# Last sequence of a hybrid Mamba, FFN and minGRU layer: the squares of both feed-forward blocks are summed on TensorE instead of on GpSimd

## The reference

```
x = x + mamba(layernorm(x))          # 256 inner channels, 16 states, conv of 4 taps
x = x + ffn(layernorm(x))            # block "a" in the kernel
x = x + min_gru_block(layernorm(x))  # 512 wide
x = x + ffn(layernorm(x))            # block "d", the same weights as "a"

def ffn(x):                          # ternary weights, 128 -> 512 -> 128
    h = gelu(ternary_linear(x, w_up))
    return ternary_linear(h, w_down)

def ternary_linear(x, w):
    rms = sqrt(sum(x * x, axis=-1)) / sqrt(d)
    return (x / (rms + 1e-8)) @ w_q.T
```

## Time and profile before

| | |
|---|---|
| median of 3 runs | 870.47 us (866.34 to 874.72) |
| the profiled execution | 870.38 us |
| its span, first to last instruction | 868.6 us |
| PE busy | 706.7 us (81%) |
| DVE busy | 677.0 us (78%) |
| ACT busy | 641.6 us (74%) |
| POOL busy | 590.9 us (68%) |
| mean granted TensorE clock | 0.904 |
| POOL L593, all 8 units | x48, 61.1 us, 1273 ns each |

### The profile page before, as it was taken

One profiled execution on the slowest core, in us unless ns is written; L12 is line 12 of the kernel. 1 busy time (PEld: TensorE's weight loads), 2 busy tenths in 40 slices (PEclk: granted clock), 3 DMA queues, 4 the chain that ended last, 5 costly groups with the idle time before them and its releaser, 6 DMA issues. The chain is left out here.

```text
span 868.6 us, 12461 instructions
## 1 busy us (share of the span) xinstructions
PE 706.7 (81%) x4060; PEld 594.6 (68%) x4060; DVE 677.0 (78%) x1059; ACT 641.6 (74%) x966; POOL 590.9 (68%) x375
## 2 busy tenths in 40 slices
PE   6446664789878997999788987999789977996975
PEld 5234553668767885778676876788667866785764
DVE  4379988869987998879977998799888997753231
ACT  4775669697789968996879778987898479616313
POOL 3178967776778877787868697888777576615312
PEclk9685776889989998999889998999899979999996
DMA  2541221112111211121111211121112111000000
GB/s 47 146 143 45 74 74 49 51 48 63 37 41 44 89 39 47 39 67 56 37 51 47 75 37 50 38 74 37 49 38 73 50 36 38 13 1 2 13 1 12
DMA packets 35185, 42.79 MB, mean 49 GB/s; under 512 B 7457, under 2 KB 17074, under 8 KB 35122
## 3 DMA queue, kind: packets, MB, share of 16 engines
q1 hardware_dynamic: 35122, 42.00, 15.9%
HBM read 39.63 MB, written 2.36 MB: 48 GB/s over the span
## 5 line engine op out<-in xcount | busy, mean ns | idle before, releaser
L441 POOL TENSOR_TENSOR inflow<-dtu,b_all 128x1024 f32<-128x1024 f32 x127 | 307.4, 2424 | 85.9 <-DVE state L1006 53.4
L1006 DVE TENSOR_TENSOR_SCAN state<-dA,inflow 128x512 f32<-128x512 f32 x256 | 298.4, 1207 | 31.2 <-ACT dA L771 27.8
L771 ACT ACTIVATE dA<-dt,decay_c 128x512 f32<-128x512 f32 x256 | 169.8, 685 | 56.6 <-DVE state L1006 55.7
L1023 DVE TENSOR_TENSOR state<-state,c_ps 128x1024 f32<-128x1024 f32 x128 | 155.5, 1215 | 22.4 <-PE c_ps L1305 18.8
L1314 PE MATMUL y_ps<-ident,state 128*128 128x128 f32 x1024 | 151.2, 297 | 0.0
L1314 PEld LDWEIGHTS y_ps<-ident,state 128*128 128x128 f32 x1024 | 135.7, 156 | 11.9 <-issue 3.8
L1201 PE MATMUL work<-in_hi,wzh_hi 128*128 128x512 f32 x256 | 103.6, 405 | 5.6 <-issue 4.3
L1305 PE MATMUL c_ps<-xd,pick 128*128 128x512 f32 x128 | 65.0, 508 | 46.0 <-DVE state L1023 45.7
L1203 PE MATMUL work<-in_lo,wzh_hi 128*128 128x512 f32 x256 | 101.0, 394 | 0.0
L1202 PE MATMUL work<-in_hi,wzh_lo 128*128 128x512 f32 x256 | 101.0, 394 | 0.0
L593 POOL TENSOR_TENSOR wide<-wide 128x512 f32<-128x512 f32 x48 | 61.1, 1273 | 27.5 <-ACT wide L818 25.0
(11 more groups left out here) (166 smaller groups left out, 1491.6 us busy)
## 6 DMA issues: line engine op xcount, KB each, us to landing
b_all<-b_scratch SPq DMA_DIRECT2D x128, 256.0 KB, 3.1
x_tok<-in_x SPq DMA_DIRECT2D x8, 256.0 KB, 3.8
out_x<-x_tok SPq DMA_DIRECT2D x8, 256.0 KB, 3.7
wide<-in_Wz SPq DMA_DIRECT2D x1, 1024.0 KB, 6.4
wide<-in_Wh SPq DMA_DIRECT2D x1, 1024.0 KB, 8.7
skip_f<-in_W SPq DMA_DIRECT2D x2, 256.0 KB, 5.7
dtu<-in_W_in SPq DMA_DIRECT2D x1, 256.0 KB
b_scratch<-gated SPq DMA_DIRECT2D x8, 32.0 KB, 1.6
```

The lines of the kernel that those rows point to most:

```text
L441: eng.tensor_tensor(inflow[:, n % 2, :, tok(b)], dtu[:, :, tok(b)], b_all[:, n % RING, tok(b)].unsqueeze(1).broadcast_to([P, HALVES, TO[b] ...
L771: act.activation(dA[:, h, tok(b)], dt[:, b % 2, h, tok(b)], ACT.Exp, scale=decay_c[:, h, n:n + 1]).then_inc(s_dA[h], 1)
L1006: dve.tensor_tensor_scan(state[:, g % 3, h, tok(b)], dA[:, h, tok(b)], inflow[:, n % 2, h, tok(b)], first, ALU.mult, ALU.add).then_inc(s_s ...
L1023: dve.tensor_tensor(state[:, g % 3, :, tok(b)], state[:, g % 3, :, tok(b)], c_ps[:, tok(b)].unsqueeze(1).broadcast_to([P, HALVES, TO[b] - ...
```

## The change

For t = N - 1 = 7 alone, POOL's `ffn_sum` does nothing, in both blocks. PE's `ffn_sumsq` of that unit multiplies all four blocks of squares by the column of ones and accumulates in PSUM: 4 blocks times 4 token tiles are 16 products, which are 32 matmuls with 32 weight loads. It waits for each square in turn on `s_sq[c]` instead of once on `s_sqsum[c]`. For the other units the count of products stays 4; only their start flag is now set on the first alone.

```
             def ffn_sum(t, c, k):
+                if t == N - 1:
+                    return
                 pool.wait_ge(s_sq[c], FB * t + k + 1)
...
             def ffn_sumsq(t, c):
                 p = c + ".sumsq"
-                pe.wait_ge(s_sqsum[c], 3 * t + 3)
+                if t < N - 1:
+                    pe.wait_ge(s_sqsum[c], 3 * t + 3)
                 bank_free(t, p)
-                for j in tiles(t):
-                    last = pe.matmul(bank(p)[:, j:j + 1], square[:, 0, cols(j)], ones[:, 0:1], start=True, stop=True)
+                terms = FB if t == N - 1 else 1
+                for k in range(terms):
+                    if t == N - 1:
+                        pe.wait_ge(s_sq[c], FB * t + k + 1)
+                    for j in tiles(t):
+                        last = pe.matmul(bank(p)[:, j:j + 1], square[:, k, cols(j)], ones[:, 0:1],
+                                         start=(k == 0 and j == tiles(t)[0]), stop=(k == terms - 1),
+                                         skip_group_check=True)
                 last.then_inc(*made(p))
```

## The result

| | before | changed |
|---|---|---|
| median of 6 runs | 870.41 us (866.34 to 875.53) | 884.11 us (874.96 to 889.6) |
| ratio | | 1.0123, 95% interval 1.0065 to 1.0182 |
| the profiled execution | 870.38 us, span 868.6 | 889.6 us, span 887.2 |
| mean granted clock | 0.904 | 0.889 |

The kernel became slower by 13.7 us in the median and by 1.2% in the ratio (10.7 us), where +4.8 us had been forecast. The range ended at 880.0.

The account below looks back on a forecast made before the run. PE was taken as the engine on the path in both blocks of unit 7, POOL's sums as hidden. Block "a" 2.15 plus block "d" 2.68 gave 4.83 us on 870.38 us, so 875.2 us, range 870.4 to 880.0.

Parts of the forecast that it names:

- What bounds the place: Unit 7, both blocks: PE's queue holds the products with ones; POOL's sums are ready 1.15 and 0.32 us earlier.
- The price of the pairs and the waits: Unit 7's sums on PE: 24 added pairs cost 2.68 us a block; the waits cost 0, at most 0.1 us.
- the bound of 0.211: Added pairs at the half clock: 0.211 us each, 5.1 us for 24, from part 0 of the down projection.
- Block "a" on the path, 2.15 us: Unit 7, block "a": 0.53 us of the added 2.68 is absorbed before DVE's read, 2.15 us go through.
- Both partners of the stretch behind it: Behind block "a": POOL's root and unit 6's sums and products all shift by 2.15 us; no slack takes it back.
- Block "d", 2.68 us: Unit 7, block "d": part 1 of the down projection and DVE's last operation start 2.68 us later; up to 5.1 plus.
- Rival B: The clock stays low through the end: +7.0 us in block "d", +9.2 with block "a", 879.6 us; chance 0.09.
- The forecast's own sign of being wrong: At the program's end: among the listed signs, a granted clock of 0.50 beyond 866 us would show the forecast wrong.
- Rival A: POOL's sums were the bound in unit 7: -1.42 us in block "a", +0.45 in "d", 869.4 us; chance 0.06.
- Rival C: Unit 7's added products are nearly free, weight loads hidden: 870.4 us; chance 0.05.

Follow-up runs that it names:

- e5: The changed kernel once more, unedited, beside the kernel before; median 882.77 us, ratio 1.0116 to the kernel before.
- e1: The kernel before with the change in block "a" of unit 7 alone, block "d" summed by POOL; median 878.81 us, ratio 1.0072.
- e3: The changed kernel with 128 columns of ones as moving operand in unit 7, both blocks, in place of one; 879.03 us, ratio 1.0058 to the kernel before.
- e7: The changed kernel with unread 128-column identity products filling PE's gaps in the last 90 us; median 874.70 us, ratio 1.0022 to the kernel before.
- e8: The changed kernel with block "d"'s sums in unit 7 moved behind both parts of the down projection; 882.96 us, ratio 1.0108 to the kernel before.
- e6: The kernel before with unread 128-column identity products filling PE's gaps in the last 90 us; median 869.16 us, ratio 0.9962.
- e9: The kernel before with filling products in PE's gaps and 128 columns of ones in the sums of all units; median 863.53 us, ratio 0.9894.
- e2: The kernel before with the change in block "d" of unit 7 alone; median 877.72 us, ratio 1.0037.
- e10: The changed kernel with filling products in PE's gaps and 128 columns of ones in unit 7 only; 871.97 us, ratio 0.9998 to the kernel before.
- e12: The changed kernel with filling products in PE's gaps and 128 columns of ones in all units; 868.08 us, ratio 0.9961 to the kernel before.
- e4: The kernel before with only the start flag changed, set on the first product alone, in all units; median 874.58 us, ratio 1.0013.
- e11: The kernel before with 128 columns of ones in the sums of all units, no filling products; median 868.09 us, ratio 0.9943.

## Why the prediction was wrong

*What bounds the place: right.* PE was on the path in both blocks and POOL's sums were not. The products start with no idle time in front in the changed kernel, and taking the sums off POOL gave nothing back.

*The price of the pairs and the waits: right.* 32 loads took 3.65 us, 0.112 us each, with four waits among them. The forecast said 3.65. At the lower clock it was 6.95 us, (6.95 - 0.33) / 31 = 0.214 us each, against the bound of 0.211.

*Block "a" on the path, 2.15 us: right* in size, 2.16 in the changed kernel and 2.16 in e5. The step that failed stood directly behind it: "Both partners of the stretch behind it shift together" and "None of them has a fixed point to be hidden under". They don't only shift. Behind the 3.65 us of one-column products the clock falls, and the stretch up to the root of block "d" of unit 6 costs 3.15 us more. The 0.20 us in the next stretch go with that fall: it took 39.83 to 39.88 us in every profile with a fall there (changed, e1, e3, e5, e7, e8) and 39.54 to 39.67 us in the others. This loss was in no case of the prediction.

*Block "d", 2.68 us: the step that failed* is "it rises in the stretch of 862 to 863 us", "during the first 8 of L1374, so that the added 24 in block "d" come after the rise". I took the moment of the rise from the kernel before as if it belonged to the code around it, and did not ask whether the added products themselves belong to what makes it rise or lets it fall. Block "d" cost 7.29 us. e3 shows that the sum was right for products of 128 columns: 2.72.

*Rival B* described block "d" well. It gave +7.0 us there (7.29 measured) and +9.2 us in all, against 12.8 in the stretch and 10 to 11 us in the ratios. Its chance of 0.09 was far too low, and the argument against it the same mistake: "the dense stretch before the rise is the same work in the same order". It was, for 3.4 us; behind it 6.8 us of one-column products stood where 1.3 us had stood. What it describes, a block that comes later and misses the rise, is what e1 shows: the unedited block lost 2.16 us. That the delay is the reason is not shown. (By the rows the rise came 3.9 and 4.2 us after the start of the dense stretch, not 3.7 to 4.2.) How much of the 4.6 us is owed to the later block and how much to its one-column products is not separated. Rival B also lacked the place behind block "a". The forecast's own sign of being wrong, a clock of 0.50 beyond 866 us, is what came. *Rival A*, POOL as the bound, is false for these two kernels. It becomes half true once the gaps are filled: in block "d" of e6 and e9 PE waits 1.24 us for POOL, in block "a" 0.48 us. *Rival C* is false, no spacing was under 0.11 us.

The sum of the case: 2.16 + 3.35 + 2.7 + 4.6 = 12.8 us, of which 4.9 is the added work and 7.9 the clock. The ratios of the timed runs give 10 to 11 us; that in some executions the clock does rise in block "d" would account for it, but is not shown. The 7.9 us are of the two profiles, then, and not a mean of all executions.

The Trainium skill, "TensorE: Matmul & The Clock Gate", section "What's actually happening", says that the throttle is released by activity, by how busy PE has recently been. Where the stretch had 128 columns throughout the trace agrees: the clock rose in e3 and e8 and stayed in e9. With one-column products it does not, if busy is what the rows call so: PE was busy for 13.78 of 14.0 us and stayed at 0.50 (changed kernel), and it fell to 0.50 with no idle time since 788.2 us (e7).

## What to carry to other kernels

A PE that the profile shows as busy can still lose its clock, here during or right behind 32 products with one moving column (3.65 us at the full clock): when an edit adds such a stretch, price everything that follows on PE at the lower clock as well, and look at the granted clock by stretches before summing durations. Where the spacing of the products is that of their weight loads anyway, as here, try widening the moving operand to the columns that the bank has room for: with 128 it cost 0.1 us a block here (8.67 against 8.57 us in e9 and e6) and the clock stayed up in more places, though not in all (e3, block "a"). Work taken off a hidden engine and put on the one that sets the end is a loss even at its bare price, here 3.5 us with the clock held.

## What the runs showed of the hardware that was not expected

- With PE unbroken the granted clock fell in or right behind stretches of 32 one-column products: at 795.5 us in e7, 3.3 us after the first of them and 0.7 us before the last had ended, and at 861.5 us in e2. With 128 columns in the same places it fell in none of e3 (block "d"), e9, e10 and e12; in block "a" of e3 it fell 5.0 us behind them, after gaps.
- A float32 pair of load and product took 0.112 us with 1 column and with 128, at the full clock (3.65 us for 32 in the changed kernel and in e3).
- The rise at the end of the program came 17.5 to 17.7 us after POOL's root of unit 7 in the kernel before, e2, e3 and e4, where the clock had fallen 0.5 to 0.7 us after that root. Where it had fallen later, 1.6 to 1.9 us after the root (changed kernel, e1, e5, e8), it did not rise at that point; in e8 it rose 18.9 us and in e1 22.4 us after the root. The later fall is in all four profiles with 32 one-column products in block "a" of unit 7 and in none of the others without filling products but e11 (2.3 us, the rise at 19.4). So by these profiles an edit in block "a" bears on the price of block "d"; what sets the moment was not found out.
